# Routing between the first two feed-forward chunks, a packed sixth chunk, and last products in eight banks

## The chip, the cores and the metric

The kernel runs on one core of a Trainium2 chip. The metric is the device time of one execution in microseconds (us), median of several runs. Engines are TensorE (PE, its weight loads PEld), VectorE (DVE), ScalarE (ACT), GpSimd (POOL) and SyncE (SP, which here only issues DMAs). Each engine runs its own list of instructions in order; semaphores tie the lists together.

## The reference

One decoder layer on x of 2 x 512 tokens and 512 channels: a squared-score causal attention, a quantised cross-attention over 2048 context rows, and a feed-forward stage with routing. In all three a layer norm comes first and the result is added to x. What the change touches is the queries of the second and all of the third:

```python
q = _fq_sym((x @ Wq + bq) * scale, axis=-1)      # rounded to 127 steps of each row and head
...
probs = softmax(xf @ gate_w.T)                   # 8 experts
topk_p, topk_i = jax.lax.top_k(probs, 2)
comb = (one_hot(topk_i, 8) * topk_p[..., None]).sum(axis=1)
eo = einsum('eni,eci->enc', silu(xf w1) * (xf w2), w3)          # I = 352 hidden channels
y = einsum('enc,ne->nc', eo, comb)
sh = silu(xf @ sw1.T) * (xf @ sw2.T) @ sw3.T                    # shared expert, 704 channels
return x + y + sh
```

## The kernel before

Tokens lie in 8 tiles (TT) of 128. Three blocks follow each other: self-attention (to about 200 us), keys, values and queries of the cross-attention with its scores (to 832 us), and `output_and_experts` (832 us to the end).

Where precision matters, an operand is split into a rounded part and the rest (`_hi`, `_lo`), and a product is three matmuls: hi x hi, lo x hi, hi x lo. ACT makes the hi part, DVE or POOL the lo part.

Queries of the cross-attention, for tile c: POOL normalises z, PE transposes it (`turn_z`), ACT makes `c_hi` (`high_z`), DVE makes `c_lo` (`low_z`, L1032), PE projects (`queries`, L1161), DVE quantises (`quantise_queries`, L1046 to L1058), ACT triples the result (`triple`, L898), PE transposes it (`turn_queries`, L1130), ACT keeps it (`keep_queries`, L903). In the loop over c, DVE does `quantise_queries(c)` and then `low_z(c + 2)`. The block ends when the last `keep_queries` and the reciprocal at L1088 are done.

The shared expert has 704 hidden channels, in 6 chunks of 128 (`SHARED`), the sixth only half filled (64 channels, the rest zeros). `hidden(c, b)` is one chunk for one half b of the tokens: 24 matmuls, 12 into bank `h1[b]` and 12 into `h2[b]`; ACT takes silu of h1 (L1753), DVE multiplies by h2 (L1975), ACT makes `h_hi` (L1755), POOL (`chunk(c)`, for chunks 0 to 2) or DVE (`low_hidden`, for chunks 3 to 5) makes `h_lo`, and likewise the rest of the down weights (`dn_lo`). POOL's `split_up(c)` (L1831) makes the rest of the up weights. `down(group)` adds up two chunks for all 8 tiles, 6 matmuls of 128 x 512 a tile, into two banks `py` in turn; DVE adds each into the residual (`add_y` L2011, `add_last` L2006), so PE waits for a bank at every tile.

Routing: `gate(b)` gives the logits of each half (12 matmuls), ACT copies them, PE transposes them (`turn_logits`), DVE subtracts the maximum (`logits`), ACT takes the exponential (with a change of its table), DVE divides, picks the two best and counts them (`probabilities`, `choose`, `running_counts`, L1924 to L1944), PE sums the counts (`places`, L2128 to L2130), DVE makes the slot of every token (`slots`, L1948 to L1965, with `slot_ok` after L1960). Then POOL scatters the rows of z into the DRAM array `slots` by 16 indirect DMAs (L1866), waits for all of them (`scattered`), and loads them back in 23 runs of 128 rows (`zg`, L1873). Every run belongs to one expert: PE transposes it (`turn_in`, L2180), multiplies it by both up weights (`run_up`, L2192, 16 matmuls of 352 columns), transposes the hidden values (`turn_hidden`, L2203) and multiplies down (`run_down`, L2215).

Order of work in this block before: PE does hidden(0,0), gate(0), hidden(0,1), gate(1), hidden(1,0), turn_logits, hidden(1,1), hidden(2,0), hidden(2,1), places, hidden(3,0), hidden(3,1), down(0), down(1), the 23 runs, hidden(4,.), hidden(5,.), down(2). SP loads expert 0 early; chunk 3 after `dlo_ok` 1; expert 1 once all four `dn_lo` are there; expert 2 after `scattered`, expert 3 right behind it, experts 4 to 7 when down(1) is done. An expert is 2176 KB. In the runs, ACT and DVE split the weights of chunks 4 and 5. After the last run POOL gathers the two expert rows of each token (L1881, four buffers), and DVE adds them, weighted (`mix(t)`, two instructions L1996 and L1999).

Of the kernel before, what the change touches and what calls it, by code (L numbers as in the profile page):

```python
# [18 lines left out]
P = 128  # L19
# [678 lines left out]
def keys_values_queries(nc, ctxT_dram, raw0, raw0_in, wkv_in, wq_dram, wq_in, wq_views, bkv_dram, bq_dram, w_hi, w_lo, k_parts,  # L698
# [3 lines left out]
    with ExitStack() as ctx:  # L702
# [244 lines left out]
        def _(v_):  # L947
# [87 lines left out]
            def quantise_queries(c):  # L1035
# [22 lines left out]
                nc.vector.tensor_scalar(q1[:, c % 2, :, :], kf[:, :, :], MAGIC, MAGIC, ALU.add, ALU.subtract).then_inc(q1_ok, 1)  # L1058
                v_.wait_ge(q1_ok, c + 1)
# [13 lines left out]
            for c in range(1, TT):  # L1073
                quantise_queries(c)
                if c + 2 < TT:
                    low_z(c + 2)
# [429 lines left out]
LATE = 1  # L1506
LAST_RUN = [min(TOKENS // P * (e + 1), RUNS - E_N + e + 1) - 1 for e in range(E_N)]
# [6 lines left out]
def output_and_experts(nc, gate_dram, rank_dram, starts_dram, w_dram, experts_dram, slots_dram, y_dram, out_dram, x_res, mv,  # L1514
# [3 lines left out]
    with ExitStack() as ctx:  # L1518
# [111 lines left out]
        po = h1  # L1630
        pl = pc[0][:, 0:TT * E_N].rearrange("p (t e) -> p t e", t=TT)
# [62 lines left out]

        def hidden_number(c, b):

            return 2 * c + b + (RUNS if c >= FIRST else 0)

        @block.sync
        def _(sp):  # L1700
# [15 lines left out]
            sp.wait_ge(dlo_ok, RAW)  # L1716
            sp.wait_ge(late_dlo_ok, 1)
# [21 lines left out]
        def _(act):  # L1739
            def split_up(c):  # L1740
                act.wait_ge(w_in[c % RAW], 16 * (c // RAW + 1))
                if 2 <= c < FIRST:
                    act.wait_ge(h2_ok, 2 * c - 2)
                nc.scalar.copy(up_hi(c).rearrange("p a k n -> p (a k n)"), raw(c)[:, 0:2 * C]).then_inc(uhi_ok, 1)
# [3 lines left out]

            def hidden(c):
                for b in range(2):  # L1750
                    n = hidden_number(c, b)
                    act.wait_ge(h1_ok, n + 1)
                    nc.scalar.activation(act_s(c)[:, b, :], h1[b][:, :], ACT.Silu).then_inc(s_ok, 1)  # L1753
                    act.wait_ge(g_ok, n + 1)
                    nc.scalar.copy(h_hi(c)[:, b * HALF_T:(b + 1) * HALF_T], g(c)[:, b, :]).then_inc(hhi_ok, 1)  # L1755
# [72 lines left out]
        def _(pool):  # L1828
# [30 lines left out]
            for c in range(FIRST - 1):  # L1859
                split_up(c + 1)  # L1860
                chunk(c)

# [23 lines left out]
        def _(v_):  # L1886
# [80 lines left out]
            def hidden(c, b):  # L1967
                n = hidden_number(c, b)
                v_.wait_ge(s_ok, n + 1)
                v_.wait_ge(h2_ok, n + 1)  # L1970
                if c not in (0, FIRST):
                    v_.wait_ge(hhi_ok, 2 * c + b - 1)
                if 0 < c <= RAW:
                    v_.wait_ge(hlo_ok, 2 * c + b - 1)
                nc.vector.tensor_tensor(g(c)[:, b, :], act_s(c)[:, b, :], h2[b][:, :], ALU.mult).then_inc(g_ok, 1)  # L1975

            def low_hidden(c, b):
                v_.wait_ge(hhi_ok, 2 * c + b + 1)
                cols = slice(b * HALF_T, (b + 1) * HALF_T)
                nc.vector.tensor_tensor(h_lo(c)[:, cols], g(c)[:, b, :], h_hi(c)[:, cols].bitcast(F32),  # L1980
# [7 lines left out]
            def low_up(c):  # L1988
                v_.wait_ge(uhi_ok, c + 1)
                nc.vector.tensor_tensor(up_lo(c).rearrange("p a k n -> p (a k n)"), raw(c)[:, 0:2 * C],  # L1990
                                        up_hi(c).rearrange("p a k n -> p (a k n)").bitcast(F32),
# [11 lines left out]
            def add_last(t):  # L2003
                v_.wait_ge(y_ok, SUMS + RUNS + t + 1)
                v_.wait_ge(mixed_ok, t + 1)
                nc.vector.tensor_tensor(x_res[:, t, :], x_res[:, t, :], py[t % 2][:, :], ALU.add).then_inc(final_ok, 1)  # L2006
# [27 lines left out]
            hidden(0, 1)  # L2034
            hidden(1, 0)
# [305 lines left out]
```

## Time and profile before

| | |
|---|---|
| time of 3 runs | 1181.31 us median (1179.78 to 1183.09) |
| profiled execution | 1178.96 us, its span 1177.2 us |
| busy share of the span | PE 83%, DVE 70%, ACT 55%, POOL 28% |
| mean granted TensorE clock | 0.970 |
| queries of the cross-attention | about 315 to 362 us |
| last block | 832 to 1177 us, of it the 23 runs 947 to 1138 us |

Matmuls are pipelined: a row's duration is from its issue to its end, so two starts give the pace. The clock is 1.00 for the full level (2.4 GHz) and 0.50 for the lower one (1.2 GHz). In a timeline, the bracket at the end of a row is the idle time of the engine before it and what ended it.

### The profile page before, as it was taken

To read this page: it belongs to the slowest core of one execution; us is meant where nothing else is said; L and a number is where in the kernel's file an instruction comes from. 1 tells how busy PE (TensorE), PEld (TensorE's weight loads), DVE (VectorE), ACT (ScalarE), POOL (GpSimd) and SP (SyncE) were. 2 spreads that over 40 slices of the span, in tenths; PEclk is the share of its full clock that TensorE was granted. 3 is DMA by queue.
4 is the path that set the end of the run, shared out by engine and by line. 5 is a ranking of instruction groups with operands and counts; after the bars stand their busy time and mean duration, and the time that the engine had idled before them with its cause. 6 is when DMAs were issued, how large, how long until landed. Compare 5 with 4: busy or idle time off the path is not lost. (4 is left out here: it accounts for less than half of the span.)

```text
span 1177.2 us, 21799 instructions
## 1 busy us (share of the span) xinstructions
PE 978.4 (83%) x8049; PEld 668.0 (57%) x8049; DVE 823.2 (70%) x1386; ACT 645.2 (55%) x1040; POOL 325.8 (28%) x313
## 2 busy tenths in 40 slices
PE   4988988999896777777767676767899989999998
PEld 3754744788673444444444444444677756565566
DVE  6748746899898999999999999999544411111126
ACT  3454252455577878888888888888333011212221
POOL 1125044565614970101010101010564500000013
PEclk9989999999997989999999999999899989999999
DMA  8400001310000030000000000000020793232125
GB/s 311 179 1 1 1 1 37 108 54 19 9 1 2 1 126 2 0 0 0 0 0 0 0 0 0 0 0 0 3 77 27 256 426 117 63 116 72 54 70 180
DMA packets 24857, 68.18 MB, mean 58 GB/s; under 512 B 2722, under 2 KB 6818, under 8 KB 23778
## 3 DMA queue, kind: packets, MB, share of 16 engines
q1 hardware_dynamic: 20114, 52.48, 11.9%
q0 software_dynamic: 4400, 14.42, 3.9%
q8 instruction: 37, 0.61, 0.2%
q10 hardware_dynamic: 288, 0.52, 0.2%
q14 instruction: 18, 0.15, 0.0%
HBM read 49.07 MB, written 18.35 MB: 57 GB/s over the span
## 5 line engine op out<-in xcount | busy, mean ns | idle before, releaser
L1333 ACT ACTIVATE cs_p_int<-cs_s_b,cs_bias,cs_step_now 128x1024 int16<-128x1024 f32 x128 | 154.1, 1204 | 63.6 <-DVE cs_bias L1368 63.5
L1361 DVE TENSOR_REDUCE cs_top<-cs_s_b 128x1 f32<-128x512 f32 x256 | 164.8, 686 | 13.1 <-PE cs_s_b L1390 4.5
L1390 PE MATMUL cs_s_b<-k_parts,q_int 96*128 96x512 bf16 x256 | 81.3, 401 | 110.1 <-ACT cs_p_int L1333 109.9
L1398 PE MATMUL cs_tp<-ident,cs_p_int 128*128 128x128 f16 x2048 | 160.8, 223 | 2.7 <-ACT cs_pT L1339 1.1
L1349 DVE TENSOR_REDUCE cs_top<-cs_s_a 128x1 f32<-128x1024 f32 x128 | 155.5, 1215 | 4.2 <-PE cs_s_a L1390 4.2
L1333 ACT ACTIVATE cs_p_int<-cs_s_a,cs_bias,cs_step_now 128x1024 int16<-128x1024 f32 x128 | 152.8, 1194 | 0.0
L1398 PEld LDWEIGHTS cs_tp<-ident,cs_p_int 128*128 128x128 f16 x2048 | 123.1, 99 | 49.3 <-issue 45.5
L2192 PE MATMUL ff_h<-ff_experts,ff_zgT 128*128 x368 | 114.9, 466 | 0.9 <-ACT ff_zgT L1761 0.9
L1390 PE MATMUL cs_s_a<-k_parts,q_int 96*128 96x512 bf16 x256 | 79.9, 395 | 22.1 <-ACT cs_p_int L1333 17.6
L1390 PEld LDWEIGHTS cs_s_b<-k_parts,q_int 96*128 (+1 forms) x256 | 15.0, 99 | 133.2 <-ACT cs_p_int L1333 124.9
L2192 PEld LDWEIGHTS ff_h<-ff_experts,ff_zgT 128*128 128x128 f32 x368 | 69.2, 193 | 36.6 <-issue 3.3
L1376 DVE COPY cs_pT<-cs_tp 128x1024 int16<-128x1024 int16 x128 | 87.1, 681 | 3.2 <-PE cs_tp L1398 3.1
L1426 PEld LDWEIGHTS cs_out<-v_int,cs_pT 128*128 128x128 f16 x2048 | 70.5, 96 | 31.5 <-issue 1.7
L1483 POOL TENSOR_TENSOR p_step<-z_sum 128x16 f32<-128x16 f32 x8 | 1.7, 212 | 308.6 <-DVE stage L1380 308.6
L2057 DVE TENSOR_TENSOR ff_run_g<-ff_run_s,ff_h 128x352 f32<-128x352 f32 x23 | 12.0, 522 | 99.4 <-ACT ff_run_s L1814 82.8
L1339 ACT COPY cs_pT<-cs_tp 128x512 int32<-128x512 int32 x128 | 74.9, 585 | 7.6 <-PE cs_tp L1398 6.8
L1426 PE MATMUL cs_out<-v_int,cs_pT 128*128 128x32 f16 x2048 | 71.6, 177 | 0.8 <-DVE cs_pT L1376 0.8
L2215 PE MATMUL ff_py<-ff_experts,ff_gT 128*128 x138 | 63.2, 593 | 0.8 <-DVE ff_gT L2018 0.8
L1814 ACT ACTIVATE ff_run_s<-ff_h 128x352 f32<-128x352 f32 x23 | 10.7, 464 | 90.2 <-PE ff_h L2192 90.2
L1873 POOL DMA_DIRECT2D ff_zg<-slots x23 | 12.7, 550 | 162.8 <-PE ff_pc L2180 158.2
L251 POOL TENSOR_TENSOR stage<-stage,mask 128x512 f32<-128x512 f32 x32 | 40.3, 1275 | 60.9 <-ACT stage L322 60.9
L2017 DVE COPY ff_gT<-ff_pc 128x256 f32<-128x256 f32 x23 | 9.8, 425 | 61.1 <-PE ff_pc L2203 61.1
(288 smaller groups left out, 2166.8 us busy)
## 6 DMA issues: line engine op xcount, KB each, us to landing
ff_experts<-in_experts_dram SPq DMA_DIRECT2D x8, 2176.0 KB, 14.8
slots<-sa_zero SPq DMA_DIRECT2D x1, 5888.0 KB, 24.7
ff_zg<-slots POOLq DMA_DIRECT2D x23, 256.0 KB, 2.9
run_y<-ff_yv SPq DMA_DIRECT2D x23, 256.0 KB, 2.0
ff_raw<-in_weights_dram SPq DMA_DIRECT2D x6, 768.0 KB, 5.0
ck_raw<-in_ctxT_dram SPq DMA_DIRECT2D x8, 512.0 KB, 3.4
stage<-in_cwkv_dram SPq DMA_DIRECT2D x2, 1024.0 KB, 5.1
out_dram<-x_res SPq DMA_DIRECT2D x8, 256.0 KB, 2.0
```

The lines of the kernel that those rows point to most:

```text
L251: pool.tensor_tensor(diag, diag, mask[:, :].unsqueeze(1).broadcast_to([P, GH, P]), ALU.mult).then_inc(masked, 1)
L1333: nc.scalar.activation(p_int[:, u, half * HALF:(half + 1) * HALF], s[:, :], ACT.Exp, bias=bias[:, u:u + 1], scale=step_now[:, h:h + 1], ac ...
L1339: nc.scalar.copy(pT[:, u, HKT:KT, :].rearrange("p k q -> p (k q)").bitcast(I32), tp[:, :, :].rearrange("p k q -> p (k q)").bitcast(I32)).t ...
L1349: nc.vector.tensor_reduce(top[:, u, 0:1], s_a[u][:, :], AX_X, ALU.max).then_inc(max_ok, 1)
L1361: nc.vector.tensor_reduce(top[:, u, 1 + c:2 + c], s_b[:, c * 512:(c + 1) * 512], AX_X, ALU.max).then_inc(max_ok, 1)
L1376: nc.vector.tensor_copy(pT[:, 1 - u, 0:HKT, :], tp[:, :, :].bitcast(I16)).then_inc(ra_ok, 1)
L1390: ins = nc.tensor.matmul(s[:, c * 512:(c + 1) * 512], q_int[0:3 * D, t, h, :], k_parts[0:3 * D, h, keys:keys + 512], start=True, stop=True)
L1398: ins = nc.tensor.transpose(tp[:, k, :], p_int[:, u, key:key + P].bitcast(F16), ident16[:, :])
L1426: ins = nc.tensor.matmul(out[:, head * D:(head + 1) * D], pT[:, u, k, :].bitcast(F16), v_int[:, k, head * D:(head + 1) * D], start=(k == 0 ...
L1873: nc.gpsimd.dma_start(zg[:, u % 2, :], run_rows(slots_dram, u)).then_inc(zg_in[u % 2], 16)
L2192: ins = nc.tensor.matmul(out[u % 2][:, 0:I_W], zgT[:, u % 2, k, :], w, start=(k == 0), stop=(k == CK - 1))
L2215: ins = nc.tensor.matmul(py[u % 2][:, :], gT[0:rows, u % 2, j, :], w, start=(j == 0), stop=(j == DN - 1))
```

## The change

Four things are altered. (1) In the queries, `low_z(c + 2)` stands inside `quantise_queries(c)`, behind the reduction, and the two small instructions that keep the step stand at its end. (2) In the last block gate(1) stands ahead of hidden(0,1), turn_logits ahead of hidden(1,0), places ahead of hidden(2,1); ACT takes the logits and the exponential between chunks 0 and 1, DVE makes the choice ahead of hidden(1,1) and the slots ahead of hidden(2,1). The rest of chunk 2 (`h_lo`, `dn_lo`) is made by DVE, not by POOL, and expert 1 waits for counts that answer to that. (3) Chunk 5 has its 64 gate columns and 64 up columns in one set of 128 weights, so hidden(5,b) is 12 matmuls into h1 alone; its `h_lo` lies in the lower 64 rows of `h_hi`, so its down product is 2 matmuls a tile, not 3. (4) `down(2)` becomes `down_last`: the 8 tiles have a bank each, tiles 0 to 3 get chunk 4 first, then chunk 5, and tiles 4 to 7 follow. The mixes are spread as (0), (1,2), (3), (4,5) over hidden(4,0) to hidden(5,1).

```diff
@@ quantise_queries(c), DVE
                 link(nc.vector.tensor_reduce(rstep[:, :], kf[:, :, :], AX_X, ALU.max, apply_absolute_value=True))
+                if 1 <= c < TT - 2:
+                    low_z(c + 2)
...
-                nc.vector.tensor_scalar(q_step[:, c, :], step[:, c % 2, :], scale, None, ALU.mult)
-                nc.vector.tensor_scalar(q_nstep[:, c, :], step[:, c % 2, :], -scale, None, ALU.mult)
...
                 nc.vector.tensor_scalar(q1[:, c % 2, :, :], kf[:, :, :], MAGIC, MAGIC, ALU.add, ALU.subtract).then_inc(q1_ok, 1)
+                nc.vector.tensor_scalar(q_step[:, c, :], step[:, c % 2, :], scale, None, ALU.mult)
+                nc.vector.tensor_scalar(q_nstep[:, c, :], step[:, c % 2, :], -scale, None, ALU.mult)
@@ SP
-            sp.wait_ge(dlo_ok, RAW)
-            sp.wait_ge(late_dlo_ok, 1)
+            sp.wait_ge(dlo_ok, EARLY)
+            sp.wait_ge(late_dlo_ok, FIRST - EARLY)
             sp.wait_ge(ulo_ok, FIRST)
             expert(1)
@@ ACT
-            hidden(0)
-            split_down(0)
+            half_hidden(0, 0)
             for b in range(2):
                 act.wait_ge(lgT_ok, b + 1)
                 nc.scalar.copy(lgT[:, b * HALF_T:(b + 1) * HALF_T], pc[b][0:E_N, :]).then_inc(lgT_read, 1)
+            half_hidden(0, 1)
+            split_down(0)
+            act.wait_ge(sub_ok, 1)
+            nc.scalar.activation(lg[:, :, :], lg[:, :, :], ACT.Exp).then_inc(exp_ok, 1)
             split_up(2)
             hidden(1)
             split_down(1)
-            act.wait_ge(sub_ok, 1)
-            nc.scalar.activation(lg[:, :, :], lg[:, :, :], ACT.Exp).then_inc(exp_ok, 1)
@@ POOL
-            for c in range(FIRST - 1):
+            for c in range(EARLY):
                 split_up(c + 1)
                 chunk(c)
+            split_up(FIRST - 1)
@@ hidden(c, b), DVE
+                gates = h2[b][:, :] if rows == P else h1[b][rows:2 * rows, :]
@@ DVE
             hidden(0, 1)
+            logits()
             hidden(1, 0)
-            hidden(1, 1)
-            logits()
-            hidden(2, 0)
             probabilities()
             choose(0)
             choose(1)
             running_counts()
+            hidden(1, 1)
+            hidden(2, 0)
+            slots()
+            low_hidden(2, 0)
             hidden(2, 1)
-            slots()
+            low_down(2)
+            low_hidden(2, 1)
...
-                    for t in ((0,), (1, 2), (3, 4), (5,))[2 * (c - FIRST) + b]:
+                    for t in ((0,), (1, 2), (3,), (4, 5))[2 * (c - FIRST) + b]:
@@ PE
+            def down_last():
+                pe.wait_ge(y_read, SUMS + RUNS)
+                pe.wait_ge(late_hlo_ok, 2 * (FIRST - EARLY) + 2)
+                pe.wait_ge(late_dlo_ok, SHARED - EARLY)
+                for t in range(TT // 2):
+                    down_part(FIRST, t)
+                pe.wait_ge(late_hlo_ok, 2 * (SHARED - EARLY))
+                for t in range(TT // 2):
+                    down_part(FIRST + 1, t).then_inc(y_ok, 1)
+                for t in range(TT // 2, TT):
+                    down_part(FIRST, t)
+                    down_part(FIRST + 1, t).then_inc(y_ok, 1)
...
             gate(0)
+            gate(1)
             hidden(0, 1)
-            gate(1)
+            turn_logits()
             hidden(1, 0)
-            turn_logits()
             hidden(1, 1)
             hidden(2, 0)
+            places()
             hidden(2, 1)
-            places()
             hidden(3, 0)
             hidden(3, 1)
             down(0)
...
-            down(2)
+            down_last()
```

`down_part(c, t)` is three matmuls for chunk 4 and two for chunk 5, into bank `sums[t]`, where `sums` is py, pc, then the four banks of h1 and h2.

## Rows read from the trace of the kernel before

**Rows 1.** Chain of work that ended last, pieces in time: start, us, what.

```profile
864.94 5.48 PE ff_h L2147 x24
...
932.32 5.32 DMA slots<-ff_z,ff_slot_i
...
937.92 8.71 DMA ff_zg<-slots
...
973.43 4.74 PE ff_h L2192 x16
```

**Rows 2.** Timeline of DVE in the last queries: start, us, line, idle before.

```profile
344.84 0.69 DVE L1048 TENSOR_REDUCE ck_rstep<-ck_kf 128x16 f32<-128x512 f32 x1
...
347.99 0.69 DVE L1032 TENSOR_TENSOR ck_c_lo<-ck_vb,ck_c_hi 128x512 fp32r<-128x512 f32 x1
...
353.40 0.69 DVE L1046 TENSOR_TENSOR ck_kf<-ck_kb,ck_raw 128x512 f32<-128x512 f32 x1 [1.56 <-PE ck_kb L1161]
```

**Rows 3.** Timeline of PE in the same stretch.

```profile
348.74 0.80 PE L1161 MATMUL ck_kb<-wq_hi,ck_c_hi 128*128 128x512 f32 x1 [2.24 <-DVE ck_c_lo L1032]
```

**Rows 4.** Timeline of ACT in the same stretch, its last two copies.

```profile
358.06 3.62 ACT L903 COPY q_int<-ck_tr 96x2048 bf16<-96x2048 bf16 x2
```

**Rows 5.** Timeline of PE, 899 to 957 us.

```profile
899.27 0.39 PE L2147 MATMUL ff_h<-zT_hi,ff_up_hi 128*128 128x512 f32 x1
...
906.71 0.41 PE L2128 MATMUL ff_pc<-ff_seen,mask 128*128 128x64 f32 x2 [1.84 <-DVE ff_upto L1944]
...
946.68 1.11 PE L2180 MATMUL ff_pc<-ident,ff_zg 128*128 128x128 f32 x4 [3.71 <-DMA ff_zg<-slots]
948.67 7.03 PE L2192 MATMUL ff_h<-ff_experts,ff_zgT 128*128 x16 [0.87 <-ACT ff_zgT L1761]
```

**Rows 6.** Stretches of 2 us: length, PE busy, granted clock, DMA share, GB/s.

```profile
908.00:910.00 2.00, 2.00 (x7) 0.61 0.00 0
910.00:912.00 2.00, 2.00 (x6) 0.54 0.00 0
...
946.00:948.00 2.00, 1.11 (x4) 0.50 1.00 428
```

**Rows 7.** Timeline of DVE in the slots, 907 to 913 us.

```profile
907.96 1.29 DVE L1950 TENSOR_SCALAR ff_ends<-ff_ends 128x8 f32<-128x8 f32 x1
909.28 1.20 DVE L1951 TENSOR_TENSOR ff_ends<-ff_ends 128x8 f32<-128x8 f32 x1
...
912.22 0.18 DVE L1960 CAST ff_slot_i<-ff_slot_f 128x16 uint32<-128x16 f32 x1
```

**Rows 8.** Timeline of POOL, 898 to 910 us.

```profile
898.54 2.40 POOL L1831 TENSOR_TENSOR ff_up_lo<-ff_raw,ff_up_hi 128x1024 fp32r<-128x1024 f32 x1 [0.50 <-ACT ff_up_hi L1744]
...
907.94 1.29 POOL L1839 TENSOR_TENSOR ff_h_lo<-ff_g,ff_h_hi 128x512 fp32r<-128x512 f32 x1 [4.82 <-ACT ff_h_hi L1755]
```

**Rows 9.** Timeline of SP, 920 us to the runs: its DMA issues.

```profile
923.00 21.82 SPq L1705 DMA_DIRECT2D ff_experts<-in_experts_dram  x7
```

**Rows 10.** POOL's DMA queue in 927:929, then in 933:935: packets, MB, share.

```profile
q0 software_dynamic: 14, 0.06, 7.8%
...
q0 software_dynamic: 263, 0.84, 104.0%
```

**Rows 11.** The loads of the 23 runs (tile `ff_zg`), issue to landing.

```profile
DMA to landing us min/median/max: 2.8/2.9/11.8
```

**Rows 12.** Timeline of DVE from 1154 us to the end.

```profile
1154.70 0.69 DVE L1975 TENSOR_TENSOR ff_g<-ff_s,ff_h 128x512 f32<-128x512 f32 x1 [0.46 <-PE ff_h L2147]
1156.07 0.69 DVE L1980 TENSOR_TENSOR ff_h_lo<-ff_g,ff_h_hi 128x512 fp32r<-128x512 f32 x1 [0.69 <-ACT ff_h_hi L1755]
1156.68 0.74 DVE L1996 SCALAR_TENSOR_TENSOR x_res<-ff_chosen,ff_p_top,x_res 128x512 f32<-128x512 f32 x1
...
1158.13 0.74 DVE L1996 SCALAR_TENSOR_TENSOR x_res<-ff_chosen,ff_p_top,x_res 128x512 f32<-128x512 f32 x1
...
1174.04 0.69 DVE L2006 TENSOR_TENSOR x_res<-x_res,ff_py 128x512 f32<-128x512 f32 x1 [0.67 <-PE ff_py L2171]
```

More of the change, by code:

```diff
@@ L1074, in _ @@
                 quantise_queries(c)
-                if c + 2 < TT:
-                    low_z(c + 2)
                 if c <= HG:
@@ L1506 @@
 LATE = 1
+EARLY = 2
+TAIL = SHARED_W - (SHARED - 1) * P
+assert 2 * TAIL == P
 LAST_RUN = [min(TOKENS // P * (e + 1), RUNS - E_N + e + 1) - 1 for e in range(E_N)]
@@ L1630, in output_and_experts @@
         po = h1
+        sums = py + pc + [h1[0], h2[0], h1[1], h2[1]]
         pl = pc[0][:, 0:TT * E_N].rearrange("p (t e) -> p t e", t=TT)
@@ L1693, in output_and_experts, with rows_of, up_parts @@
         assert SHARED - FIRST == GROUP and FIRST == RAW + 1
+        def rows_of(c):
+            return P if c < SHARED - 1 else TAIL
+        def up_parts(c):
+            return 2 if c < SHARED - 1 else 1
         def hidden_number(c, b):
@@ L1743, in split_up, with half_hidden @@
                     act.wait_ge(h2_ok, 2 * c - 2)
-                nc.scalar.copy(up_hi(c).rearrange("p a k n -> p (a k n)"), raw(c)[:, 0:2 * C]).then_inc(uhi_ok, 1)
+                width = up_parts(c) * C
+                nc.scalar.copy(up_hi(c).rearrange("p a k n -> p (a k n)")[:, 0:width], raw(c)[:, 0:width]).then_inc(uhi_ok, 1)
             def split_down(c):
                 nc.scalar.copy(dn_hi(c), raw(c)[:, 2 * C:3 * C]).then_inc(dhi_ok, 1)
-            def hidden(c):
[L1750 to L1755, printed above, removed]
+            def half_hidden(c, b):
+                n = hidden_number(c, b)
+                act.wait_ge(h1_ok, n + 1)
+                rows = slice(0, rows_of(c))
+                nc.scalar.activation(act_s(c)[rows, b, :], h1[b][rows, :], ACT.Silu).then_inc(s_ok, 1)
+                act.wait_ge(g_ok, n + 1)
+                nc.scalar.copy(h_hi(c)[rows, b * HALF_T:(b + 1) * HALF_T], g(c)[rows, b, :]).then_inc(hhi_ok, 1)
+            def hidden(c):
+                half_hidden(c, 0)
+                half_hidden(c, 1)
             def turned(u):
@@ L1979, in low_hidden @@
                 cols = slice(b * HALF_T, (b + 1) * HALF_T)
-                nc.vector.tensor_tensor(h_lo(c)[:, cols], g(c)[:, b, :], h_hi(c)[:, cols].bitcast(F32),
+                rows = slice(0, rows_of(c))
+                low = h_lo(c)[rows, cols] if rows_of(c) == P else h_hi(c)[TAIL:P, cols]
+                nc.vector.tensor_tensor(low, g(c)[rows, b, :], h_hi(c)[rows, cols].bitcast(F32),
                                         ALU.subtract).then_inc(late_hlo_ok, 1)
@@ L2005, in add_last @@
                 v_.wait_ge(mixed_ok, t + 1)
-                nc.vector.tensor_tensor(x_res[:, t, :], x_res[:, t, :], py[t % 2][:, :], ALU.add).then_inc(final_ok, 1)
+                nc.vector.tensor_tensor(x_res[:, t, :], x_res[:, t, :], sums[t][:, :], ALU.add).then_inc(final_ok, 1)
             def add_y(group):
@@ L2143, in hidden @@
                 cols = slice(b * HALF_T, (b + 1) * HALF_T)
-                for m, (out, made) in enumerate(((h1, h1_ok), (h2, h2_ok))):
+                for m, (out, made) in enumerate(((h1, h1_ok), (h2, h2_ok))[0:up_parts(c)]):
                     for k in range(CK):
@@ L2151, in down @@
             def down(group):
-                early = min(GROUP * (group + 1), RAW)
+                early = min(GROUP * (group + 1), EARLY)
                 late = GROUP * (group + 1) - early
@@ L2173, in down, with down_part @@
                     ins.then_inc(y_ok, 1)
+            def down_part(c, t):
+                tile = slice(t * P, (t + 1) * P)
+                if rows_of(c) == P:
+                    pairs = ((h_hi, dn_hi), (h_lo, dn_hi), (h_hi, dn_lo))
+                else:
+                    pairs = ((h_hi, dn_hi), (h_hi, dn_lo))
+                for i, (hh, w) in enumerate(pairs):
+                    ins = nc.tensor.matmul(sums[t][:, :], hh(c)[:, tile], w(c),
+                                           start=(c == FIRST and i == 0), stop=(c == SHARED - 1 and i == 1))
+                return ins
+            def down_last():
[10 more added lines that the diff above has]
+                    down_part(FIRST + 1, t).then_inc(y_ok, 1)
             def turn_in(u):
@@ L2317, in _arrays @@
           for s in ("sw1", "sw2")]
-    a["weights"] = np.concatenate([*up, chunks(f("L0_ffn_sw3").T)], axis=2)
+    last = [u[SHARED - 1].reshape(P, CK, P) for u in up]
+    both = np.concatenate([w[:, :, 0:TAIL] for w in last], axis=2).reshape(P, C)
+    up = [np.concatenate([u[0:SHARED - 1], w[None]]) for u, w in zip(up, (both, np.zeros_like(both)))]
+    down = chunks(f("L0_ffn_sw3").T)
+    down[SHARED - 1, TAIL:P] = down[SHARED - 1, 0:TAIL]
+    a["weights"] = np.concatenate([*up, down], axis=2)
     rows = np.stack([f("L0_ffn_w1"), f("L0_ffn_w2")], axis=1)
```

20 lines of the change are left out of this document (9 added, 11 removed).

## The prediction, made before the change was run

> **What bounds the kernel now.** First the chain of work that ended last, read back from the end. From 947 us on it is PE almost throughout, 4.74 us for the up products of each run [rows 1]. Just ahead of the runs it is not PE but routing: the last scatter takes 5.32 us from its issue to landing, then the first load of a run 8.71 us [rows 1], and PE idles 3.71 us for it [rows 5]. Then the timelines of each engine around the places that the diff touches, to see who is late there. PE had waited for routing once before, 1.84 us ahead of places [rows 5], and was granted only 0.61 and 0.54 of its clock in the 4 us from 908 on [rows 6]. So there are three places where time can move: the end of the queries (ACT and DVE last), the road from logits to the first run (two chains side by side, PE's products and POOL's scatter), and the tail behind the runs. The scores between them keep their own pace and only begin earlier or later; so do the runs. The sum is made against the profiled execution, 1178.96 us (span 1177.2), and is then taken from the median, 1181.31, which lies 2.35 us higher.
>
> **Queries.** DVE is never idle in the middle of this loop, and the move takes no work from it, so the middle keeps its pace. The last tile is another matter: low_z(7) runs at 347.99, PE starts the last projection behind it at 348.74 after 2.24 us of idleness [rows 3], and DVE idles 1.56 us for that [rows 2]. In the new order low_z(7) follows the reduction that ends at 344.84 + 0.69 = 345.53, so the projection can start some 2 us earlier, PE has not idled and is no slower for it, and the 1.56 us vanish: the last quantisation follows the one before it at once. The two small instructions behind the rounding, of the kind that takes 0.18 us [rows 7], add 0.1 to 0.2 us for ACT. What is late next is ACT: its copies of 1.86 us end the block, the last two as 3.62 [rows 4]; with the triples of tiles 6 and 7 (1.47 each, no gap) they end some 1.6 us earlier. low_z now delays the rounding of its own tile by 0.61 less 0.17 us; ACT's triple waits for that, and in the middle it has over 1 us of slack. Taken: 1.6 us; bounds 1.2 and 1.75.
>
> **Routing, PE's side.** The products are the same (24 matmuls 5.48 us [rows 1], so 0.228 each). What goes is the idleness ahead of places: from the end of hidden(2,1), 899.27 + 5.44 = 904.71, to 906.71, is 2.0 us; and the low clock behind it, (1 - 0.61) x 2 + (1 - 0.54) x 2 = 1.7 us. New waits in the way: hidden(1,0) waits for nothing of routing; ACT changes its table ahead of silu(1,0), which makes g(1,0) some 0.3 us later, but PE wants it only 5 us later, ahead of hidden(2,0). The choice on DVE now stands ahead of g(1,1); DVE starts it near 889 and needs 19 small instructions of about 0.24 us (0.18 for the smallest kind [rows 7]), 4.6 us, plus one stall of up to 1.2 [rows 7], so to 894.8, and PE wants the result (places) at 899.2 and g(1,1) at 899.9. 4.4 us of slack cover that; if they were gone, PE would idle again as before. hidden(3,0) needs POOL's split of chunk 3, by 901, and starts at 905. So PE leaves down(1) at 942.97 - 3.7 = 939.2 (942.97 is the start of its idle time, 946.68 - 3.71 [rows 5]).
>
> **Routing, POOL's side.** Places moves ahead of hidden(2,1), from 906.71 to 899.2 [rows 5], 7.5 us earlier. The slots are made behind it. L1950 and L1951 took 1.29 and 1.20 us, not 0.2, and the first ended with POOL's instruction that had started at 907.94 [rows 7, 8]: DVE stood still while POOL worked. Those two stalls, 2.1 us, go, since chunk 2's rest is now DVE's, behind the slots; but POOL's split of chunk 3 (2.40 us [rows 8]) now falls on the slots, since ACT's split comes only behind copy(1,1) and the down weights, near 897.4: POOL works from 898.6 to 901.0, and DVE stands from about 900.2 on. L1950 then runs at 901.0; two clean instructions, and the 1.9 us from 910.48 to 912.40 [rows 7]: 903.5 against 912.40, 8.9 us earlier. The trace has no stall longer than 1.1 us; were that the limit, slots would be 0 to 0.3 us earlier. The Trainium skill, SBUF — State Buffer (section SBUF: two separate sides), says that GpSimd and VectorE share a port pair and that the one that comes first holds it for its whole instruction; by it the stall lasts to the end of the 2.40 us, which speaks against this place for the slots. The sum changes by 0.3 us on a chain with slack, as the next step shows.
>
> The 16 scatters are issued 19.6 us long as before, the last at 923.4 (before, 932.32 [rows 1]). But they do not land at that pace. SP issues expert 1 at 923.00 [rows 9], and while it moves, POOL's queue gets 0.06 MB in 2 us, later 0.84, that is 0.42 MB/us [rows 10]: the eight scatters issued behind expert 1, of 0.26 MB each, wait for it and then need 5.0 us; the last landed 14.6 us behind expert 1's issue (937.64, from 932.32 + 5.32). Expert 1 is tied to low_down(3), which is tied to hidden(3,1): it moves by PE's 3.7 us only, to 919.3. But by then twelve scatters are out and only four are stuck, 2.5 us less behind it: 919.3 + 14.6 - 2.5 = 931.4; with a little less traffic under expert 1 I take 931.0, against 937.64. The first load of a run goes out at 931.3 behind experts 2 and 3, and with the same 8.71 us [rows 1] lands at 940.0. PE is free at 939.2: the two chains nearly meet, and the DMA is the later one by 0.8 us.
>
> **The runs' start.** turn_in(0) moves from 946.68 [rows 5] to 940.0: 6.7 us (7.5 if PE were the later one). PE then hasn't idled for 3.71 us, and the clock, 0.50 at 946 [rows 6], should be full: 4.74 + 0.16 [rows 1] against 7.03 us [rows 5] for the first products, 0.6 us for the transposes and 0.1 behind: 2.8 us. Taken together 9.5 us; bounds 6.7 (low clock all the same) and 10.3. Loads 1 to 3 took at most 11.8 us under the experts [rows 11] and are wanted 11 to 15 us after their issue; experts 4 to 7 go out 3.7 us earlier, as PE leaves down(1). No cost. The later runs keep their pace, 8.08 us each; the splits of chunk 5 shrink, beside PE.
>
> **Tail.** PE loses 24 matmuls in hidden(5,.) (5.4 us) and 8 in the down products (1.8), and its waits for banks. But DVE becomes the bound. In the old order g(5,0) started at 1154.70 after 0.46 us of idleness [rows 12], so behind the mixes at 1154.2; now its product is ready at 1152, and it starts there. From 1154.15, by the row starts: g to low 1.37, low to mix 0.61, a mix 1.45 [rows 12]: mix(3) ends at 1157.6; g(5,1) and low 1.98: 1159.55; mix(4), mix(5): 1162.45; two adds at 0.67 (0.69 less the overlap [rows 12]): 1163.8; mix(6): 1165.25; two adds: 1166.6; mix(7): 1168.05; four adds: 1170.7. PE is done by 1166.4: it has 12 of chunk 4's matmuls behind it at 1157.4, idles 2.4 us for low(5,1), and needs 28 x 0.228. The last add ended at 1174.04 + 0.69 = 1174.73: 4.0 us. The last four output DMAs now come every 0.67 us, not 1.37, 256 KB each, near the 428 GB/s of [rows 6]: up to 0.5 us back. Taken: 3.8; bounds 3.2 and 4.6. The gathers for mixes 6 and 7 land by 1162.3 and 1165, ahead of their use.
>
> **Sum.** 1.6 + 9.5 + 3.8 = 14.9 us. 1178.96 - 14.9 = 1164.1 in a profiled execution; 1181.31 - 14.9 = 1166.4 as a median.
>
> **Rivals.** (A) The scatters do not gain on expert 1: both queues share the same engines, expert 1 moves by 3.7 us only, and the last scatter still lands 14.6 us behind it, at 934. Then load 0 comes at 942.9, PE idles 3.7 us as before, the clock falls as before, and routing gives 3.7, not 9.5: 1181.31 - 9.1 = 1172.2. For it: POOL's queue starves as long as an expert moves. Against it: half the bytes are left behind it. Chance 0.14. (B) The clock falls though PE hardly idles, once ahead of turn_in(0) and once behind it: 2.8 us less, 1169.2; for it the 1.84 us that cost clock [rows 5, 6]. 0.14. (C) The choice on DVE ahead of g(1,1) is over 4.4 us longer than counted, or POOL's split of chunk 3 comes late behind it, and PE stalls at hidden(2,0) to (3,0) with a low clock: 3 to 5 us less, 1169 to 1171. 0.05. (D) Slower than before: the loads of runs. Their latency under the experts was up to 11.8 us, and they have 11 to 15; experts 4 to 7 (8.7 MB, 20 us) now start with the first run, not 3.7 us ahead. It decides from about 15 us of latency on: each us beyond is lost in two or three loads, and with a low clock in each gap (2.3 us). Only from 20 us on, on three loads, is more lost than the 14.9 gained: 3 x (5 + 2.3) = 22, 1188. The trace's longest is 11.8 [rows 11]. Chance 0.02. (E) The change does less than it says, since DVE bound both ends: queries give nothing (the ACT copies end it anyway) and the tail 2.5: 1169.3. 0.05. Forecast 0.60.
>
> **How the numbers follow.** A measurement tells about 0.3%, 3.5 us, from no change. All cases but D are faster by more than that: 0.97 with some of the rest; D has 0.02, and 0.01 is left for the same. The range: down to 1162.0 (all upper bounds, 1.75 + 10.3 + 4.6 = 16.7, and a median nearer to its lowest run), up to 1171.5, which takes in B, C, E and half of the way to A. The forecast's own range is 1164 to 1169.
>
> **What would show it.** Queries: DVE's last L1046 without idleness, scores starting at 360.5. Routing: places near 899, no wait of PE there, clock 1.00 from 865 to the runs, POOL's first scatter near 903.5 less 1.6, expert 1 at 919 less 1.6, load 0 landing within 2 us of PE's end of down(1). Tail: DVE without a gap from g(5,0) to the last add. Wrong if the first run starts later than 8 us after the last scatter's landing, or if any run waits for its load.

## The result, and the profile after

The changed kernel takes 1168.36 us in the median of 4 runs (1166.94 to 1170.5), the kernel before, run beside it, 1180.82 (1179.78 to 1183.09): 0.9894 of it, 95% interval 0.9875 to 0.9912, so 12.5 us less. Forecast were 1166.4 us, with 1162.0 to 1171.5 as the range and 14.9 us as the gain.

The first rows of its page, then PE's in the page of before. The shares hardly differ (before, PE 83% and DVE 70%), since PE's busy time fell along with the span, by 12.5 us with 32 matmuls less; they don't say where the time went.

```profile
span 1167.6 us, 21732 instructions
PE 965.9 (83%) x8017; PEld 660.7 (57%) x8017; DVE 821.3 (70%) x1389; ACT 645.2 (55%) x1040; POOL 322.5 (28%) x310
...
PE 978.4 (83%) x8049; PEld 668.0 (57%) x8049; DVE 823.2 (70%) x1386; ACT 645.2 (55%) x1040; POOL 325.8 (28%) x313
```

So the two traces were cut at six marks: DVE's bias sum of query tile 1 (its second L1046), the first product of the scores, the first product of hidden(0,0), the first transpose of run 0, the first product of hidden(4,0), the end of the last add. Each column sums to its span. The last three columns are the unedited kernel again (E1, E8, E9 below), the second is the kernel before once more (E10).

| stretch, us | before | E10, before | after | E1 | E8 | E9 |
|---|---|---|---|---|---|---|
| start to query tile 1 (untouched) | 323.92 | 323.94 | 325.13 | 322.75 | 323.67 | 324.94 |
| to the scores | 38.13 | 36.58 | 35.45 | 35.44 | 35.45 | 35.45 |
| to hidden(0,0) (untouched) | 502.65 | 503.01 | 501.87 | 501.55 | 502.53 | 502.04 |
| to run 0's transpose | 81.98 | 80.89 | 80.30 | 75.76 | 78.49 | 75.31 |
| to hidden(4,0) | 191.02 | 191.52 | 188.46 | 190.21 | 188.46 | 188.52 |
| to the end of the last add | 37.03 | 37.01 | 33.61 | 33.03 | 33.99 | 33.00 |
| to the end of the span | 2.47 | 2.55 | 2.78 | 2.76 | 2.81 | 2.74 |

The spans of "before" and "after" are 9.6 us apart, less than the medians (12.5): the profiled execution of before was 1.9 us under its median, that of the changed kernel 1.0 us over. All three parts of the change gain in the column "after", but the fourth row only 1.7 us of some 6. The timeline of PE around places (the small products that add up the counts) shows that the planned part worked: no idleness (before, 1.84 us [rows 5]).

```profile
897.03 0.33 PE L2154 MATMUL ff_pc<-ff_seen,mask 128*128 128x64 f32 x2
```

The loss is in the first down products. The timeline of DVE there (the bracket is the idle time before the row and what ended it), then that of PE:

```profile
916.63 0.68 DVE L2007 TENSOR_TENSOR ff_dn_lo<-ff_raw,ff_dn_hi 128x512 fp32r<-128x512 f32 x1
918.85 0.69 DVE L2034 TENSOR_TENSOR x_res<-x_res,ff_py 128x512 f32<-128x512 f32 x1 [1.53 <-remote]
922.37 0.69 DVE L2034 TENSOR_TENSOR x_res<-x_res,ff_py 128x512 f32<-128x512 f32 x1 [2.84 <-PE ff_py L2192]
924.52 0.69 DVE L2034 TENSOR_TENSOR x_res<-x_res,ff_py 128x512 f32<-128x512 f32 x1 [1.46 <-remote]
```

```profile
919.59 0.50 PE L2192 MATMUL ff_py<-ff_dn_hi,ff_h_hi 128*128 128x512 f32 x1 [2.66 <-DVE x_res L2034]
923.11 0.79 PE L2192 MATMUL ff_py<-ff_dn_hi,ff_h_hi 128*128 128x512 f32 x1 [1.11 <-DVE x_res L2034]
```

DVE could have made its first sum at 917.3, behind L2007; it made three of them late, PE had only two banks and waited, and then ran at a lower clock, as the stretches show (length, then PE's busy time; the clock, third figure from the right, is 0.72 in the second):

```profile
908.00:920.00 12.00, 9.34 (x42) 7.43 (x41) 4.05 (x6) 2.36 (x4) 8.96 (x11) 1.00 0.62 215
920.00:932.00 12.00, 10.89 (x37) 8.26 (x36) 4.12 (x6) 0.00 (x0) 2.85 (x4) 0.72 0.74 264
```

No step of the forecast has this. The fifth row gained 2.56 in return: PE came so late that load 0 was there, it did not idle at turn_in(0), and the clock stayed full: run_up(0) took 5.00 us, not 7.03 [rows 5].

### The profile page after: what moved, and what is told of

Read it like the earlier page. It is cut to its first block and busy times, and to the rows that moved or that the text cites. A ratio compares the mean times of both kernels' runs of the same rounds, so it can differ in the third digit from the quotient of the medians.

```text
span 1167.6 us, 21732 instructions
## 1 busy us (share of the span) xinstructions
PE 965.9 (83%) x8017; PEld 660.7 (57%) x8017; DVE 821.3 (70%) x1389; ACT 645.2 (55%) x1040; POOL 322.5 (28%) x310
## 5 line engine op out<-in xcount | busy, mean ns | idle before, releaser
L251 POOL TENSOR_TENSOR stage<-stage,mask 128x512 f32<-128x512 f32 x32 | 40.3, 1276 | 61.3 <-ACT stage L322 61.3
```

What stands on the lines that cost most here:

```text
L251: pool.tensor_tensor(diag, diag, mask[:, :].unsqueeze(1).broadcast_to([P, GH, P]), ALU.mult).then_inc(masked, 1)
```

## The experiments

Twelve runs in three comparisons; each comparison ran on a chip of its own with the kernel before beside it. Two theories of the late sums stood at the start: either they belong to that one execution, and the forecast's mechanism holds; or they come from the new order, in which expert 1's load moves beside scatters and sums. Times from a mark, as "39.09 us behind hidden(0,0)", are taken within one trace. The rivals of the forecast still open were B (the clock falls though PE hardly idles) and E (queries and tail give less).

### First chip: E1 to E4 (before: 1176.44 us)

**E1, the changed kernel unedited.**

> The changed kernel once more. In its first trace DVE took the first three sums of down(0) 1.5, 2.8 and 1.5 us late with their products long done, PE idled 2.7 + 1.1 us for them and had a low clock for 6 us: 5.5 us. Theory 1 (the late sums belong to the order of the work, expert 1 now goes out while scatters are still issued): they are in this trace too, at the same place within 1 us, and the median is 12 to 13 us below the kernel before. Theory 2 (they belong to that one execution): this trace has sums 0.7 us behind each product as before, PE leaves down(1) 3.5 to 4 us earlier against hidden(0,0) than in the kernel before, and the runs spread over 5 us with the lowest near 1164.

1162.39 us (1159.56 to 1164.6), ratio 0.9881 [0.9859, 0.9904]. No sum was late. POOL's first scatter began 39.09 us behind the first product of hidden(0,0), before 48.02: 8.93 earlier (forecast 8.9); the last one landed 6.24 earlier (6.6). PE idled 1.00 us at turn_in(0) (0.8), and then rival B came true: the stretches behind it have clock 0.73 and 0.50 (third figure from the right).

```profile
935.50 0.66 PE L2225 MATMUL ff_pc<-ident,ff_zg 128*128 128x128 f32 x4 [1.00 <-DMA ff_zg<-slots]
937.03 6.39 PE L2237 MATMUL ff_h<-ff_experts,ff_zgT 128*128 x15 [0.87 <-ACT ff_zgT L1776]
```

```profile
937.00:939.00 2.00, 1.97 (x5) 1.32 (x6) 0.00 (x0) 0.00 (x0) 0.00 (x0) 0.73 1.08 457
939.00:941.00 2.00, 2.00 (x4) 1.04 (x4) 0.00 (x0) 0.00 (x0) 0.00 (x0) 0.50 1.01 427
```

**E2, queries as before.**

```diff
-                if 1 <= c < TT - 2:
-                    low_z(c + 2)
+                nc.vector.tensor_scalar(q_step ...)      # the two small ones back ahead of the reciprocal
...
+                if c + 2 < TT:
+                    low_z(c + 2)                         # back behind quantise_queries(c)
```

> Only the queries' part is undone (low_z behind the quantisation, the two small instructions ahead of the reciprocal). If the prediction's step holds: DVE idles 1.5 us ahead of its last bias sum, the scores start 1.5 us later than in the changed kernel, and the time is 1.3 to 1.8 us longer. Rival: the scores swallow a shift of their start (they are held by ACT, and PE's clock is low at their start), then the same time within 0.5.

1162.38 us (1160.94 to 1166.9), ratio 0.9893 [0.987, 0.9916]. The medians of E1 and E2 are equal, as the rival expected. The trace shows the step all the same: 38.15 us from query tile 1 to the scores, as before (38.13), against 35.44 in E1. The stretch of the scores behind it is 1.26 us shorter here than in E1 (500.29), but with the same order of the queries it took 502.65 in before and 503.01 in E10: it scatters, and that it swallows a shift is not shown. So no median shows the 2.7 us in the whole time. And E2's turn_in(0) shows that B is not a rule: 0.83 us of idleness, full clock.

```profile
934.92 0.66 PE L2225 MATMUL ff_pc<-ident,ff_zg 128*128 128x128 f32 x4 [0.83 <-DMA ff_zg<-slots]
936.46 5.00 PE L2237 MATMUL ff_h<-ff_experts,ff_zgT 128*128 x16 [0.87 <-ACT ff_zgT L1776]
```

**E3, routing as before**: EARLY = 3, places, logits, choice, slots and ACT's order back; new queries and tail.

```diff
-EARLY = 2
+EARLY = 3
...
-            places()
             hidden(2, 1)
+            places()
```

> Only the routing's order is undone (gate, turn_logits, places, the choice, the slots, chunk 2's rest on POOL); queries, the packed chunk and the tail stay changed. The prediction's terms give 9.5 us for routing without the late sums, about 4 to 6.5 with them. So: 4 to 6.5 us slower than the changed kernel if the late sums are in its ordinary execution, 9 to 10 if they are not. Its trace should have sums 0.7 us behind their products in down(0), and PE idle 3.7 us ahead of the first run.

1170.29 us (1167.6 to 1173.23), ratio 0.9953 [0.9936, 0.9971]. From hidden(0,0) to run 0 82.10 us and on to hidden(4,0) 191.02, both as before; PE waits 3.76 us at turn_in(0) again. Routing is worth 1170.29 - 1162.39 = 7.9 us, queries and tail together 6.15. Without late sums 9 to 10 were expected; the 1.7 us of E1's low clock at run 0 are most of what is missing.

**E4, expert 1 behind the scatters.**

```diff
-            expert(1)
             sp.wait_ge(scattered, 16 * TOP * TT)
+            expert(1)
             expert(2)
```

> The changed kernel, but expert 1 goes out only when all scatters have landed. Theory 1a (expert 1's transfer beside POOL's scatters makes DVE late): the late sums vanish, PE leaves down(1) 5 us earlier, the last scatter lands 2.7 us behind its issue, near 924, and the first run starts about 5 us earlier: 4 to 5.5 us faster than the changed kernel. Rival 1b (DVE is late for another reason, as its own instructions' fetch or POOL's scatters alone): the sums are late at the same place, PE leaves down(1) as late as now, and the time is the same within 0.7.

1160.49 us (1160.34 to 1161.57), ratio 0.9869 [0.9847, 0.989]. In E1 and E4 the last scatter's issue and the first load's:

```profile
918.58 0.96 POOL L1883 DMA_INDIRECT slots<-ff_z,ff_slot_i  x1 [0.31 <-issue]
926.72 1.18 POOL L1890 DMA_DIRECT2D ff_zg<-slots  x2 [7.18 <-DMA slots<-ff_z,ff_slot_i]
```

```profile
920.08 0.96 POOL L1883 DMA_INDIRECT slots<-ff_z,ff_slot_i  x1 [0.30 <-issue]
923.08 1.19 POOL L1890 DMA_DIRECT2D ff_zg<-slots  x2 [2.04 <-DMA slots<-ff_z,ff_slot_i]
```

The wait behind the last scatter shrinks from 7.18 to 2.04 us. Load 0 is then there before PE, which doesn't idle at turn_in(0) (74.37 us behind hidden(0,0), which is PE's own pace) and keeps its clock. On the late sums this run says nothing, since E1 on the same chip had none to take away: neither the 4 to 5.5 us of 1a nor the "same within 0.7" of 1b came out.

### Second chip: E5 to E8 (before: 1178.77 us)

**E5, chunk 5 unpacked.** `rows_of` gives P, `up_parts` 2, weights as before; eight banks and mixes stay.

```diff
         def rows_of(c):
-            return P if c < SHARED - 1 else TAIL
+            return P
         def up_parts(c):
-            return 2 if c < SHARED - 1 else 1
+            return 2
```

> The changed kernel with one part undone: chunk 5 is again two full sets of up products and three down products per tile (24 + 8 matmuls more, 7.3 us of PE at 0.228 each); the eight banks and the mixes between the chunks stay. Measured from the first product of hidden(4,0) to the end of the last add: 37.03 us in the kernel before, 33.03 in the repeat of the changed kernel. Theory (DVE sets the end once its inputs are there): low(5,1) comes where it came before, 24.5 us after that first product, and from its end DVE needs the same 10.8 us as in the repeat, so 35.3 us, the last four adds in one row. Rival (PE sets the end): the 32 matmuls add in full, 40.3 us. Second rival (packing is all of the tail's gain): 37.0.

1169.76 us (1168.33 to 1170.12), ratio 0.9917 [0.9898, 0.9936]. The last stretch took 39.27 us: near the 40.3 of "PE sets the end", but not for that reason. ACT's silu(5,1), whose product ended at 1146.2, came 3.7 us late. DVE's g(5,1) began 3.98 us behind the end of its products (1148.9), where g(4,0) and g(4,1) of this trace began 0.11 us behind theirs: 3.9 us late. PE then idled 3.38 us for them. The rows of ACT, DVE and PE:

```profile
1149.96 0.60 ACT L1764 ACTIVATE ff_s<-ff_h 128x512 f32<-128x512 f32 x1 [4.28 <-remote]
...
1152.92 0.69 DVE L1995 TENSOR_TENSOR ff_g<-ff_s,ff_h 128x512 f32<-128x512 f32 x1 [5.07 <-remote]
...
1155.04 0.50 PE L2203 MATMUL ff_py<-ff_dn_hi,ff_h_hi 128*128 128x512 f32 x1 [3.38 <-DVE ff_h_lo L2002]
```

39.27 less 3.9 is 35.4, beside the 35.3 of "DVE sets the end". From low(5,1) (1154.30) on DVE needs 11.56 us, in E1 (1147.23) 11.51: the order of its work is the same. That the 3.9 us are a disturbance and no part of this version is argued from these rows, and one thing speaks against a rare one: the four runs lie close together (1168.33 to 1170.12), 5.3 us above E8 in the median, just as the last stretches of the two traces differ (39.27 and 33.99). On this chip the version seems to have it in every run.

**E6, two banks**, five products a tile, each tile waiting for the add two before.

```diff
-        sums = py + pc + [h1[0], h2[0], h1[1], h2[1]]
+        sums = [py[t % 2] for t in range(TT)]
...
+                for t in range(TT):
+                    if t >= 2:
+                        pe.wait_ge(final_ok, t - 1)
+                    down_part(FIRST, t)
+                    down_part(FIRST + 1, t).then_inc(y_ok, 1)
```

> The changed kernel with the other part of the tail undone: chunk 5 stays packed, but the last down products go tile by tile, five matmuls each, into two banks, each tile waiting for the add two tiles before. Theory (DVE sets the end, and two banks only tie the last two adds to PE): first down product when low(5,1) is there, 22.2 us after the start of hidden(4,0), mixes 6 and 7 unmoved, and behind mix(7) the last two adds 1.1 us apart instead of 0.61: 34.5 us from hidden(4,0) to the last add, against 33.03 and 37.03. Rival (eight banks are what gives the gain): 36.5 or more.

1166.83 us (1165.17 to 1172.07), ratio 0.9891 [0.987, 0.9913]. The last stretch took 35.70. PE had idled 5.41 us ahead of its first down product and got 0.55 and 0.60 of its clock in the 8 us around, so that DVE waited 1.04 us for the second tile: 34.7 without that, beside 34.5 expected. But the idleness is this version's own, since it makes none of chunk 4's products ahead; whether the clock has to fall there, one trace can't say. Behind mix(7) the last two adds do hang on PE:

```profile
1163.79 1.38 DVE L2029 TENSOR_TENSOR x_res<-x_res,ff_py 128x512 f32<-128x512 f32 x2
1165.99 0.69 DVE L2029 TENSOR_TENSOR x_res<-x_res,ff_py 128x512 f32<-128x512 f32 x1 [0.82 <-PE ff_py L2203]
1167.12 0.69 DVE L2029 TENSOR_TENSOR x_res<-x_res,ff_py 128x512 f32<-128x512 f32 x1 [0.44 <-PE ff_py L2203]
```

**E7, E4 again, and E8, the changed kernel again.**

> The kernel with expert 1 behind the scatters once more, timed against the kernel before on the same chip as the next one. If expert 1 late is worth something of its own (no load beside the scatters, so the first run never waits and keeps its clock), its median is 1 to 3 us under that of the changed kernel and the first run's products take 5.0 us; if the 1.9 us between the medians of the first comparison were chance, the two are within 0.5 us.

> The changed kernel itself again, unedited. If DVE's late sums in the first group of down products come from expert 1's load beside them, they show up in this profile again, with some 5 us more from the first product of hidden(0,0) to the runs than 75.8. If they were of that one execution, there is no wait of over 0.6 us on DVE's first sums, the transposes of run 0 begin 75.5 to 76.5 us after the first product of hidden(0,0) with about 1 us of idleness, and the tail is 33.0 us.

E7 1165.35 us (1164.07 to 1167.5), ratio 0.9886 [0.9868, 0.9905]; E8 1164.43 (1163.36 to 1168.02), ratio 0.9881 [0.986, 0.9901]. Here expert 1 late gained nothing (0.9 us above E8, where 1 to 3 below or the same within 0.5 were expected), and the theory of expert 1's load falls: the sums are late in E7 too, where no expert moves beside them, by the same amounts as in E8 and E5, and nearly so in E6. DVE in E7:

```profile
914.74 0.68 DVE L2034 TENSOR_TENSOR x_res<-x_res,ff_py 128x512 f32<-128x512 f32 x1
917.78 0.69 DVE L2034 TENSOR_TENSOR x_res<-x_res,ff_py 128x512 f32<-128x512 f32 x1 [2.36 <-PE ff_py L2192]
921.32 1.45 DVE L2034 TENSOR_TENSOR x_res<-x_res,ff_py 128x512 f32<-128x512 f32 x2 [2.85 <-PE ff_py L2192]
```

The second sum comes 3.04 us behind the first in E7, 3.06 in E8, 3.07 in E5, 3.05 in E6; in E4, the same program as E7 on the first chip, it follows at once. That they belong to one execution falls too. E7 and E8 have them once more in the tail, as the profile on record has: an add whose product was done and for which DVE was free began 0.28, 1.03 and 0.52 us late, in the eight profiles of the other two chips none. DVE in E8, whose first product was done at 1152.1, and in E9, where PE's products came at the same times within 0.05 us behind hidden(4,0):

```profile
1154.83 1.29 DVE L2029 TENSOR_TENSOR x_res<-x_res,ff_py 128x512 f32<-128x512 f32 x2 [1.03 <-PE ff_pc L2203]
```

```profile
1151.49 0.69 DVE L2029 TENSOR_TENSOR x_res<-x_res,ff_py 128x512 f32<-128x512 f32 x1
```

This is why the tail took 33.99 us in E8 and 33.00 in E9. An obvious suspect is code that arrives late. The packets of the queue for instructions do not tell the two kinds of profile apart: between 895 and 935 us there is one of 16 KB, 1.7 us behind the first sum in E7 and 1.8 in E4. That is no proof, as it doesn't show what each engine waited for.

In both E7 and E8 PE is the later at turn_in(0) (78.49 us behind hidden(0,0), 4.1 more than E4's 74.37), which is why expert 1's place no longer counts.

### Third chip: E9 to E12 (before: 1174.93 us)

The four look for the cause of the late sums. E9 and E10 are the changed kernel and the kernel before, unedited; these are the edits of the other two:

```diff
@@ E11, POOL
             pool.wait_ge(slot_ok, 1)
+            pool.wait_ge(y_read, TT)
@@ E12, DVE
             low_z(TT - 1)
+            for _ in range(24):
+                link(nc.vector.memset(run_f[:, :], 0.0))
             hidden(0, 0)
```

> The changed kernel unedited, as the control of the next three on one chip. Four profiles on one chip had no late sums in the first group of down products, four on another had them all alike, the one with expert 1 late among them: DVE's second sum 3.05 us behind the first and the third 3.53 us behind the second, instead of 0.61 and 1.82. If the lateness is a matter of the chip or of the process, this run and every other of this call with the same DVE program and the same scatters agree, late or not; if it is chance in each execution, this call's profiles are mixed.

> The kernel before, unedited, on the same chip. There the first sums begin behind the ninth scatter as in the changed kernel, and expert 1 is issued at the same place. If the control's sums are late for a reason that both kernels share, they are late here too (second sum over 2 us behind the first, and some 4 us more from the first product of hidden(0,0) to the runs than 81.98); if only the new order of DVE's program brings it, they are 0.61 us apart.

> The changed kernel with POOL's scatters held back until DVE has made the first eight sums, so that no scatter is issued beside them. If POOL's issuing of scatters (it shares the way to SBUF with DVE, and stalled DVE elsewhere in this kernel) makes the sums late, they are 0.61 us apart here even where the control's are late; if it is something else, they stay late. The runs start some 25 us later in either case, which is not what is measured.

> The changed kernel with 24 tiny memsets added to DVE's program ahead of g(0,0), where it idles, so that everything behind stands 24 instructions later in DVE's program; the work beside the sums (scatters, expert 1) stays as it is. If the late sums belong to a place in DVE's program (its code arriving late there), the wait moves away from the sums, to 24 instructions ahead of them (around the slots) or out of sight, and the sums are 0.61 us apart; if they belong to what runs beside them, they are late as in the control.

E9 1163.02 us (1161.31 to 1163.82), ratio 0.9891 [0.9856, 0.9926]; single runs of E10 1177.21, E11 1185.66, E12 1163.11. On this chip no sum was late in any, E9 included:

```profile
916.87 1.28 DVE L2034 TENSOR_TENSOR x_res<-x_res,ff_py 128x512 f32<-128x512 f32 x2
919.30 0.69 DVE L2034 TENSOR_TENSOR x_res<-x_res,ff_py 128x512 f32<-128x512 f32 x1 [1.15 <-PE ff_py L2192]
```

So E11 and E12 could not tell their theories apart, and whether the kernel before has late sums on the second chip was not seen. What follows is only that in down(0) all profiles of one comparison agree: four late, twice four not. (On record the changed kernel's profile has late sums and that of before none; whether the two came from one chip is not known.) So the lateness seems to go with the chip or with how that comparison's programs lay in memory, and not with chance in each execution. E11's 22 us more are its own: PE idles 21.84 us at turn_in(0) for the scatters that were held back. E12's memsets cost nothing, and its turn_in(0) repeats E1's: idle 1.00, run_up(0) in 6.69 us.

E10 and E9 show something else, on the clock. PE's row at places in E10, and the stretch behind it:

```profile
905.51 0.41 PE L2128 MATMUL ff_pc<-ff_seen,mask 128*128 128x64 f32 x2 [1.83 <-DVE ff_upto L1944]
```

```profile
907.00:909.00 2.00, 2.00 (x10) 1.65 (x9) 1.97 (x2) 0.18 (x1) 2.00 (x2) 1.00 0.00 0
```

The same wait of 1.8 us that cost clock in the trace of before (0.61 [rows 6]) and in E3 (0.62) cost none here. The 2.28 us ahead of the last query projection didn't either: the row at 348.74 takes 0.50 us, in before 0.80 [rows 3], and DVE's 1.56 us of idleness [rows 2] are gone in the unchanged kernel. That is the 1.55 us of the table's second row between before and E10.

## Why the prediction was right, and where it was not

**The total.** 14.9 us were forecast; the medians of the four comparisons give 12.5, 14.05, 14.3 and 11.9. The sum of the profile on record is another: queries 2.7 (forecast 1.6), routing 4.2 (9.5), tail 3.1 (3.8), together 10.0; with 0.4 us lost in the untouched stretches that is the 9.6 between the two spans. Routing is short because 4.5 us were lost in the late sums (80.30 against E1's 75.76), of which a full clock at the runs gave 1.75 back. So that this total fell into the range was in part luck: routing gave less than half of its term, the queries more than its, and the medians lie 2.9 us further apart than the profiles. The medians can't be split like this: 14.3 us came out on the chip where all profiles had late sums, 14.05 and 11.9 on those where none had.

**Queries: 1.6 forecast, 2.7 measured, outside the bounds.** Two things were mis-sized. "The middle keeps its pace" is wrong: DVE went from 4.87 to 4.73 us a tile, since the two small instructions follow the rounding by 0.35 us where the next large one followed by 0.46. And the row at 345.56 took 0.77 us, not 0.17, because POOL worked until 346.30; low_z in its place lost nothing. Rows of before (DVE, POOL), then of E9:

```profile
345.56 0.77 DVE L1051 TENSOR_SCALAR ck_step<-ck_rstep 128x16 f32<-128x16 f32 x1
...
344.34 1.96 POOL L860 PARTITION_ALL_REDUCE v_step<-ck_own_top  x1 [10.87 <-DVE ck_own_top L994]
```

```profile
346.06 0.69 DVE L1032 TENSOR_TENSOR ck_c_lo<-ck_vb,ck_c_hi 128x512 fp32r<-128x512 f32 x1
346.67 0.17 DVE L1053 TENSOR_SCALAR ck_step<-ck_rstep 128x16 f32<-128x16 f32 x1
...
344.84 1.96 POOL L860 PARTITION_ALL_REDUCE v_step<-ck_own_top  x1 [10.34 <-DVE ck_own_top L994]
```

Together 1.13 us (36.58 less 35.45), with the clock full in both. The other 1.55 is what the forecast counted, the idleness ahead of the last tile; but it was the low clock that made it, so it is there only where the clock falls (before and E2, not E10).

**Routing, PE: right.** From hidden(0,0) to down(0) E1 needs 51.58 us, before 55.30: 3.72 less, forecast 3.7 (2.0 and 1.7). The 1.7 are clock again: E10 has 53.65.

**Routing, POOL: right.** Slots 8.9 earlier, as said. hidden(0,0) begins 2.25 us earlier in this trace than in that of before; with that added the choice ran from 889.3 to 894.9 (forecast 889 to 894.8), with one stall of 1.0, POOL's split of chunk 3 from 898.75 to 901.1 (898.6 to 901.0), and DVE stood until it ended:

```profile
898.09 0.83 DVE L1966 TENSOR_SCALAR ff_ends<-ff_ends 128x8 f32<-128x8 f32 x1
...
896.50 2.39 POOL L1847 TENSOR_TENSOR ff_up_lo<-ff_raw,ff_up_hi 128x1024 fp32r<-128x1024 f32 x1
```

The Trainium skill, SBUF — State Buffer (section SBUF: two separate sides), has GpSimd hold the shared port for its whole instruction; this row agrees, but no stall here is longer than 1.1 us, so the limit that the forecast left open stays open. Rival A is out: E1's scatters landed 6.24 us earlier, not 3.7.

**The runs' start: 9.5 forecast; 7.0 in E1, 9.2 in E9, 8.9 in E2** (the sums of the fourth and fifth rows against 273.00; E2 has 264.14), 4.2 on record. Against E10, whose clock stayed full at places, E9 gains 8.6. 6.7 of it, the earlier start, measured 6.2 to 6.7. The 2.8 of clock hung on little: PE idled 0.48, 0.83 or 1.00 us, and with 1.00, twice, the clock fell and took 1.7 us. The forecast gave this 0.14; E1 and E12 had it, of the four profiles with the new routing, expert 1 early and no late sums (E1, E2, E9, E12).

**A sign that was set wrong.** By the forecast, it is wrong if the first run starts later than 8 us after the last scatter's landing. It started 9.1 us after it in E1, 8.9 in E9 and 9.05 in before. The forecast's own times have 9.0 (931.0 and 940.0), so the sign contradicted them and says nothing about the mechanism.

**Tail: 3.8 forecast, 3.7 measured in E1** (37.03 less 33.03, less 0.29 at the outputs), 3.1 on record, a little under the lower bound, with one late add of 0.52 us. DVE sets the end as said: E9's tail is as short as E1's though the clock was low in its last products. As they ran, E6 (packing alone) gained 1.3 us in this stretch and E5 (eight banks alone) lost 2.2. Less E6's wait for the low clock and E5's late start, packing alone is worth some 2.4 us (37.03 - 34.7), eight banks alone 1.6 (37.03 - 35.4), both together 4.0; these two are estimates.

**Rivals D and E.** No run behind the first waited for its load. E is out on both counts.

**What stays open.** Why DVE's sums in down(0), its adds in the tail and ACT's silu in E5 came late on the second chip and in the profile on record. Neither expert 1 (E7) nor one execution's chance explains it; scatters beside the sums and a place in DVE's program were tried where the effect was absent.

**A faster version.** E4's order is 1.9 us under the changed kernel on the first chip (intervals overlap) and 0.9 above it on the second. It takes away the wait at turn_in(0): run_up(0) took 5.00 us in E4 and 4.99 in E7. It is not shown faster than the changed kernel, only faster than the kernel before: 16 us and 13.4 us.

## What to carry to other kernels

When two chains are brought to meet at one point, as PE's products and POOL's scatters here, the last microsecond between them can decide about the clock as well: aim to let the engine with the clock be the later one, for instance by moving a large load from beside the small DMAs (7.18 to 2.04 us). No median here shows what that gains, only the traces. Before an idle gap is written down as a gain, see whether the clock made it: cut at marks and compare two profiles of the same kernel first, since untouched stretches differed by up to 2.4 us (and by 4.4 us, start to query tile 1, between E2 and E6), and the medians of two versions that differ by 2.7 us in the trace came out equal. Where two engines stall each other, put the instruction there that is not held up.

## What the runs showed of the hardware that was not expected

- The same idle time of PE leaves the clock full in one execution and not in the next. Full after 0.48, 0.83, 1.83 and 2.28 us; low after 1.00 (twice, with 0.87 more behind it), 1.82, 1.84 and 2.24. The 2.6 us ahead of the last down products left it full in E1, E2, E12 and the profile on record, and in E3, E4, E7, E8, E9 and E11 it fell, at the latest 2 us behind their start. The price at run 0 was 1.7 us, in the tail nothing where DVE was the later one: 33.00 us in E9, whose clock in a stretch of them is below (0.50), 33.03 in E1.

```profile
1149.00:1151.00 2.00, 2.00 (x6) 1.53 (x5) 1.93 (x4) 0.00 (x0) 1.70 (x2) 0.50 0.67 168
```

- While POOL worked, three DVE instructions with all operands in SBUF stood until POOL's ended (0.6, 0.7 and 1.0 us lost), but a subtraction with one operand in PSUM, 346.06 in E9, took its usual 0.69. The Trainium skill, SBUF — State Buffer (section SBUF: two separate sides), names as affected only VectorE instructions in a two-port mode or with two inputs from SBUF; these rows agree, though no trace shows the mode of an instruction. By it the late sums, which have one operand in PSUM, are not POOL's doing; no run here shows that.
- On one chip of three, and in the profile on record, DVE began two or three sums 1.5 to 3.5 us late, in five profiles at the same place; ACT and DVE were late once more in E5 (3.7 and 3.9 us) and DVE in the tail of three (0.28 to 1.03 us). The same program on another chip had none of it (E4, E7).
